# A layered graph network inside a six-part kernel: gathers of 784 unpadded chunks, products over pairs of chunk and target block

## The reference, cut to what matters

```python
dinv = where(deg > 0, deg ** -0.5, 0.0)
norm = dinv[row] * dinv[col]
for l in range(5):
    edge_fea = concatenate([edge_attr[:, 3:] @ ew1[l], edge_attr[:, 0:3] @ ew2[l]], axis=-1)
    msg = norm[:, None] * (h[row] + edge_fea)
    agg = segment_sum(msg, col, num_segments=n)
    h = relu(concatenate([h, agg], axis=1) @ mlp_w[l] + mlp_b[l])
    ...  # normalised over the nodes; relu but in the last layer
```

## Time and profile before

| | us |
|---|---|
| runs of the kernel before | 14183.71, 14226.25, 14222.39 |
| their median | 14222.39 |
| the profiled execution | 14220.56 |
| its span in the trace | 14218.8 |
| POOL busy | 7369.4 (52%) |
| PE busy | 7586.1 (53%) |
| DVE busy | 6529.1 (46%) |
| ACT busy | 1314.3 (9%) |
| gathers of the layers, first to last issue, layers 0 to 4 | 1365, 1273, 1282, 1276, 1280 |

### The profile page before, as it was taken

The page is one execution under the profiler, slowest core; times in us unless marked ns, Lnnn a source line. Parts: engine busy times, 40 slices in busy tenths (PEclk is TensorE's granted clock), DMA queues, the critical chain, the costliest instruction groups (busy, mean ns, idle before and its releaser), DMA issues. The chain is left out here.

```text
span 14218.8 us, 158198 instructions
## 1 busy us (share of the span) xinstructions
PE 7586.1 (53%) x34918; PEld 5503.2 (39%) x34919; DVE 6529.1 (46%) x18936; ACT 1314.3 (9%) x3588; POOL 7369.4 (52%) x7692
## 2 busy tenths in 40 slices
PE   0002355552139677765655465555554655378877
PEld 0002344431026444444544344444443444233355
DVE  7336544411015356654444344434443444345566
ACT  0000000001001100001000100010001000123342
POOL 5772466635740255564666566656665666445400
PEclk9999866675569788877776777677776766578988
DMA  1000233211000133322333233323332333211203
GB/s 58 20 1 1 71 91 91 82 43 48 2 7 21 57 81 83 82 73 63 88 87 87 67 87 87 87 69 86 88 87 67 85 88 87 58 21 21 23 11 102
DMA packets 518785, 873.35 MB, mean 61 GB/s; under 512 B 180375, under 2 KB 355656, under 8 KB 517579
## 3 DMA queue, kind: packets, MB, share of 16 engines
q0 software_dynamic: 323968, 674.90, 18.6%
q1 hardware_dynamic: 194635, 196.60, 4.4%
HBM read 771.76 MB, written 105.62 MB: 62 GB/s over the span
## 5 line engine op out<-in xcount | busy, mean ns | idle before, releaser
L308 POOL DMA_INDIRECT p_layers_place<-nodesC,p_layers_idx x4160 | 3942.5, 948 | 2937.6 <-issue 1573.7
L393 PE MATMUL p_layers_bank<-p_layers_hots,p_layers_place 128*128 128x128 f32 x16640 | 3366.7, 362 | 2863.4 <-DVE agg L379 1513.9
L393 PEld LDWEIGHTS p_layers_bank<-p_layers_hots,p_layers_place 128*128 128x128 f32 x16640 | 2869.0, 257 | 3452.7 <-issue 1933.9
L379 DVE TENSOR_TENSOR agg<-agg,p_layers_bank 128x256 f32 x4160 | 1751.5, 421 | 2282.3 <-issue 858.9
L369 DVE TENSOR_SCALAR p_layers_hots<-iota,p_msg_edges 128x128 f32<-128x128 f32 x3328 | 997.6, 363 | 759.9 <-issue 599.8
L308 POOL DMA_INDIRECT p_gather_rows<-xn,p_gather_idx x832 | 788.3, 947 | 822.7 <-ACT p_gather_idx L302 578.6
L263 POOL DMA_INDIRECT listC<-h x782 | 777.1, 994 | 526.1 <-issue 253.0
L393 PE MATMUL p_agg_bank<-p_agg_hot,p_gather_rows 128*128 128x128 f32 x3328 | 685.9, 374 | 594.2 <-DVE agg L379 372.9
L263 POOL DMA_INDIRECT listA<-h x782 | 812.7, 1039 | 344.4 <-issue 341.0
L263 POOL DMA_INDIRECT listD<-recD,rowD x512 | 493.1, 963 | 785.3 <-issue 785.3
L393 PEld LDWEIGHTS p_agg_bank<-p_agg_hot,p_gather_rows 128*128 128x128 f32 x3328 | 602.8, 271 | 677.9 <-issue 373.6
(11 more groups left out here) (387 smaller groups left out, 8125.2 us busy)
## 6 DMA issues: line engine op xcount, KB each, us to landing
p_layers_place<-nodesC,p_layers_idx POOLq DMA_INDIRECT x4160
nodesC<-p_layers_place SPq DMA_DIRECT2D x24, 896.0 KB, 4.7
part_y<-rows SPq DMA_DIRECT2D x21, 896.0 KB
agg<-part_y SPq DMA_DIRECT2D x18, 896.0 KB, 10.3
p_gather_rows<-xn,p_gather_idx POOLq DMA_INDIRECT x832
x<-p_ffn_acc SPq DMA_DIRECT2D x14, 896.0 KB, 4.1
listA<-h POOLq DMA_INDIRECT x782
listC<-h POOLq DMA_INDIRECT x782
```

What stands on the lines that cost most here:

```text
L308: nc.gpsimd.indirect_dma_start(out=self.rows[s][:, u, :], out_offset=None, in_=self.table, in_offset=bass.IndirectOffsetOnAxis(ap=self.idx ...
L379: nc.vector.tensor_tensor(to, to, prod, ALU.add).then_inc(self.added[u], 1)
L393: ins = nc.tensor.matmul(self.bank[u][:, f * P:(f + 1) * P], self.g.rows[s][:, u, f * P:(f + 1) * P], self.hot[s][:, u, :], start=True, st ...
```

## The change

In the message network alone:

- `PackedSort` takes the place of `Sort` for this list. The windows' edges follow each other without holes, which makes `NQ` = 784 chunks. A chunk may then hold edges of two windows, so the products go over pairs (chunk, window), of which there are again up to 832. `PackedSort` makes five tables in spare words of `rows`: each pair's window (`cw`), its slot among the 16 tiles of gathered chunks (`slots`), how many sets must have landed (`landed`), how many pairs must be copied before a set's slot is free (`freed`), and for the next step each pair's chunk and window (`pair_q`, `pair_w`). Each record's place gets its window times 128 added.
- `Spread`, in the first block of `messages`, spreads the places from chunks to pairs: 7 parts, each of a transpose and products of 832 columns on PE, and a comparison and a copy on DVE.
- `FromList` and `PairAggregate` run the layers. POOL's loop has 49 turns (784 gathers) and waits for `ready[s]`, which is now the end of a DMA. SP's loop issues that DMA (`give`: 128x4 source nodes into `idx[s]`, in layer 0 also the records' raw words) after it has waited for the slot, and tells ACT of landed sets (`relay`). ACT copies each pair's 128x260 from its slot to one of two halves of 4 (`near`), and in layer 0 makes the attribute product, which was DVE's. PE reads `near`. The loops of ACT, PE and DVE keep 52 turns.
- `edges` shrinks to the source nodes (128 x 784). 16 more scatters of the second graph's list stand beside the layer norm of `messages` (`NORM_D` 60 to 76), 16 fewer in the last part.

```diff
 NC2 = chunks_of(E2)
 FIRST_A = 128
 PARTS_C = (0, 160, 138)
-PART_D, NORM_D, FIRST_D, PER_D = 40, 60, 40, (80, 58, 58, 58)
+PART_D, NORM_D, FIRST_D, PER_D = 40, 76, 40, (80, 58, 58, 58)
 EVERY, RINGS = 8, 3
 RA, RC, RD = 3, 6, 2
+NQ = -(-E1T // SU) * SU
+PAIR_ROW, PAIR_SLOT, PAIR_LAND, PAIR_FREE = 32, NC1, 2 * NC1, 2 * NC1 + NC1 // U
...
+class PackedSort(Sort):
...
+    def __init__(self, sp, sh, T, key, rec, row, one, rows):
+        tables = rows[PAIR_ROW:PAIR_ROW + 1, :].bitcast(I32)
+        super().__init__(sp, sh, T, NQ, key, rec, row, tables[:, 0:NC1], one)
+        self.slots, self.landed = tables[:, PAIR_SLOT:PAIR_SLOT + NC1], tables[:, PAIR_LAND:PAIR_LAND + NC1 // U]
+        self.freed, self.work = tables[:, PAIR_FREE:PAIR_FREE + NQ // U], tables[:, PAIR_WORK:PAIR_WORK + NC1]
+        self.pair_q, self.pair_w = rows[:, PAIR_Q:PAIR_Q + NC1], rows[:, PAIR_W:PAIR_W + NC1]
...
+    def _tables(self, nc, dve, link):
+        sh, ends, row = self.sh, self.ends[:, 1:NT + 1], slice(PAIR_ROW, PAIR_ROW + 1)
+        last, cut, begin = (self.marks[:, n, :] for n in range(3))
...
+        link(nc.vector.tensor_scalar(self.len_j, self.len_i, P - 1, None, ALU.bitwise_and))
...
+        link(nc.vector.tensor_tensor(last, self.low, cut, ALU.add))
...
+        nc.vector.sem_inc(self.marked, 1)
...
+        dve.wait_ge(self.turned, START + 3)
+        link(nc.vector.tensor_copy(self.cols, self.sums[0:NT, 128:131]))
+        link(nc.vector.tensor_copy(self.split, self.cols[:, 1:2].to_broadcast([NT, P])))
+        link(nc.vector.tensor_scalar(self.ended, sh.chunkrow[0:NT, 0:NC1], self.cols[:, 0:1], None, ALU.is_ge))
+        link(nc.vector.tensor_scalar(self.begun, sh.chunkrow[0:NT, 0:NQ:U], self.cols[:, 2:3], None, ALU.is_ge))
+        nc.vector.sem_inc(self.after_done, 1)
...
+        dve.wait_ge(self.winsum, START + 2)
+        link(nc.vector.tensor_scalar(self.pair_w, self.wide[:, 0:NC1], float(NT - 1), float(P), ALU.min, ALU.mult))
+        link(nc.vector.tensor_scalar(self.cw, self.wide[row, 0:NC1], float(NT - 1), None, ALU.min))
+        nc.vector.sem_inc(self.rows_done, 1)
...
+        dve.wait_ge(self.winsum, START + 4)
+        link(nc.vector.scalar_tensor_tensor(self.pair_q, sh.chunkrow[:, 0:NC1], 1.0 / P, self.wide[:, 0:NC1], ALU.mult,
+                                            ALU.subtract))
+        nc.vector.sem_inc(self.rows_done, 1)
+        link(nc.vector.tensor_scalar(self.pair_q, self.pair_q, float(NQ - 1), None, ALU.min))
+        link(nc.vector.tensor_copy(self.work, self.pair_q[row, :]))
+        link(nc.vector.tensor_scalar(self.slots, self.work, SU - 1, None, ALU.bitwise_and))
+        link(nc.vector.tensor_scalar(self.landed, self.work[:, U - 1:NC1:U], 2, None, ALU.arith_shift_right))
+        link(nc.vector.tensor_scalar(self.landed, self.landed, 1.0, None, ALU.add))
...
+        dve.wait_ge(self.winsum, START + 5)
+        link(nc.vector.scalar_tensor_tensor(self.freed, sh.chunkrow[row, 0:NQ:U], 1.0 / P, self.wide[row, 0:NQ // U],
+                                            ALU.mult, ALU.add))
...
+    def _tables_pe(self, nc, pe):
...
+        for n, by in enumerate((sh.ones[0:NT, :], self.split)):
+            if n:
+                pe.wait_ge(self.rows_done, START + n)
+            for b in range(0, NC1, 512):
+                m = min(512, NC1 - b)
+                nc.tensor.matmul(self.wide[:, b:b + m], by, self.ended[:, b:b + m], start=True,
+                                 stop=True).then_inc(self.winsum, 1)
+        pe.wait_ge(self.rows_done, START + 2)
+        nc.tensor.matmul(self.wide[:, 0:NQ // U], self.split, self.begun, start=True, stop=True).then_inc(self.winsum, 1)
...
+class FromList(Gather):
...
+    def pool_set(self, nc, pool, it, s):
+        pool.wait_ge(self.ready[s], it * 16 + 16)
+        hold(pool)
+        for u in range(U):
+            nc.gpsimd.indirect_dma_start(
+                out=self.rows[s][:, u, :], out_offset=None, in_=self.table,
+                in_offset=bass.IndirectOffsetOnAxis(ap=self.idx[s][:, u:u + 1], axis=0)).then_inc(self.here[s], 16)
...
+class PairAggregate(Aggregate):
...
+    HALVES = 2
...
+        self.near = [sp.sb(f"near{h}", [P, U, TW]) for h in range(self.HALVES)]
...
+    def pe_set(self, nc, pe, it, s, edge_terms):
+        near, attr = self.near[s % self.HALVES], self.attr[s % self.HALVES]
+        pe.wait_ge(self.hot_ready, START + it * S + (s + 1))
+        for u in range(U):
+            pe.wait_ge(self.copied, START + it * SU + (s * U + u + 1))
+            pe.wait_ge(self.added[u], START + it * S + s)
+            if edge_terms:
+                pe.wait_ge(self.attr_made, START + it * SU + (s * U + u + 1))
+                pe.wait_ge(self.edge_added, START + it * SU + (s * U + u + 1))
+            for f in range(FB):
+                ins = nc.tensor.matmul(self.bank[u][:, f * P:(f + 1) * P], near[:, u, f * P:(f + 1) * P],
+                                       self.hot[s][:, u, :], start=True, stop=True)
...
             ins.then_inc(self.g.used, 1)
...
+    def act(self, nc, act, l, edge_terms, zero):
+        with act.Fori(0, self.turns) as i:
+            it = l * self.turns + i
+            land = numbers_of(nc, mybir.EngineType.Activation, self.land, i * S, S, NQ // U)
+            for s in range(S):
+                near, attr = self.near[s % self.HALVES], self.attr[s % self.HALVES]
+                slots = numbers_of(nc, mybir.EngineType.Activation, self.slots, i * SU + s * U, U, SU - 1)
+                act.wait_ge(self.g.used, START + it * SU + (s * U + AHEAD - (self.HALVES - 1) * U))
+                act.wait_ge(self.landed, (land[s] & 255) + (START + l * (NQ // U)))
+                for u, slot in enumerate(slots):
+                    nc.scalar.copy(near[:, u, :], self.flat[:, ds(slot * TW, TW)]).then_inc(self.copied, 1)
+                if edge_terms:
+                    act.wait_ge(self.copied, START + it * SU + (s * U + U))
+                    hold(act)
+                    for u, slot in enumerate(slots):
+                        nc.scalar.activation(attr[:, u, :], self.raw.rearrange("p t w -> p (t w)")[
+                            :, ds(slot * RC + 2, 4)], ACT.Identity, bias=zero[:, 0:1],
+                                             scale=near[:, u, D:D + 1]).then_inc(self.attr_made, 1)
...
+    def sp(self, nc, sp, l, edge_terms):
+        def relay(i, s):
+            sp.wait_ge(self.g.here[s], (l * self.g.turns + i) * (16 * U) + 16 * U)
+            hold(sp)
+            if edge_terms:
+                sp.wait_ge(self.raw_here[s], i * 16 + 16)
+                hold(sp)
+            nc.sync.sem_inc(self.landed, 1)
+        def give(i, s, done):
+            sp.wait_ge(self.copied, done + (START + l * NC1))
+            hold(sp)
+            if edge_terms:
+                sp.wait_ge(self.attr_made, done + START)
+                hold(sp)
+            sp.dma_start(self.g.idx[s], self.g.edges[:, ds(i * SU + s * U, U)]).then_inc(self.g.ready[s], 16)
+            if edge_terms:
+                sp.dma_start(self.raw[:, s * U:(s + 1) * U, :],
+                             self.listed[:, ds(i * SU + s * U, U), :]).then_inc(self.raw_here[s], 16)
+        for s in range(S):
+            if s == S - 1:
+                relay(0, 0)
+            give(0, s, 0)
+        with sp.Fori(1, self.g.turns) as i:
+            free = numbers_of(nc, mybir.EngineType.SP, self.free, i * S - (S - 1), S, NC1)
+            for s in range(S):
+                relay(i - 1 if s < S - 1 else i, (s + 1) % S)
+                give(i, s, free[s] & 1023)
+        for s in range(1, S):
+            relay(self.g.turns - 1, s)
...
                 normalise(l)
             clear(l)
-            with act.Fori(0, self.g.turns) as i:
-                for s in range(S):
-                    self.g.act_set(nc, act, l * self.g.turns + i, i, s)
+            self.a.act(nc, act, l, l == 0, self.zero)
...
@@ -1810,6 +2023,54 @@
         nc.vector.tensor_tensor(to, to, self.turn.rearrange("p (f n) -> p f n", f=FB), ALU.add).then_inc(self.added, 1)
...
+        self.numbered, self.flipped = sp.sem("numbered"), sp.sem("flipped")
+        self.made, self.taken = sp.sem("made"), sp.sem("taken")
+        self.parts = [(k, min(P, NQ - k)) for k in range(0, NQ, P)]
+    def pe(self, nc, pe):
+        def flip(n):
+            k, m = self.parts[n]
+            nc.tensor.transpose(self.turn[0:m, n % 2, :], self.numbers[:, k:k + m],
+                                self.sh.ident).then_inc(self.flipped, 1)
+        flip(0)
+        for n, (k, m) in enumerate(self.parts):
+            pe.wait_ge(self.made, START + 2 * n + 2)
+            if n + 1 < len(self.parts):
+                flip(n + 1)
+            for b in range(0, NC1, 512):
+                c = min(512, NC1 - b)
+                ins = nc.tensor.matmul(self.sums[:, b:b + c], self.turned[n % 2][0:m, :],
+                                       self.picks[n % 2][0:m, b:b + c], start=(n == 0),
```

(17 more changed lines are left out.)

167 lines of the change are left out of this document (123 added, 44 removed).

## The result

The changed kernel took 14792.91 us (median of four, 14741.26 to 14820.99) beside 14205.36 us for the kernel before: 1.041 of it, 95% interval 1.0374 to 1.0445. The forecast was 14312 us, with 14530 as the end of the range: right in sign, far too small in size. Two later comparisons gave 1.0445 (1.0417 to 1.0473) and 1.0432 (1.0386 to 1.0479).

The account below looks back on a forecast made before the run. POOL's stops for used sets and DVE's slow phases beside POOL's runs were taken as the bound. Profiled 14220.6 + 12 tables + 20 spread + 4 starts + 48 layers 1 to 4 + 7 layer 0 = 14312 us; range 13950 to 14530.

Parts of the forecast that it names:

- What bounds the kernel: Layers: gathered rows lie ready; POOL stops for want of used sets, DVE is slow at 0.3 pace during POOL's runs.
- The release and the stop: Layers 1 to 4: freeing a slot through copies and index DMA takes 3.75 us, making POOL's stop 4.9 us.
- The cycle, n = (g + 4.27) / 2.90: Layers 1 to 4: sets per POOL run n from stop g; at 4.9 us n = 3.16, a layer 1284 us.
- Layers 1 to 4: Gather layers after the first: 12 us more each, +48 in all, from -8 to +120, upper end +160.
- Layer 0: First gather layer, DVE relieved of the attribute product: +7 us, from -98 to +57.
- The tables: Some 25 DVE operations and a second row product on PE: +12 us, from 0 to 25.
- Spread: After the norm in the messages' first block, seven parts on PE, plus pick and sum: +20 us, from 11 to 24.
- The 16 scatters: Beside the messages' norm: 20 us of POOL, hidden behind its 40.9 us wait for the block's end.
- The last part: End of the kernel: gains nothing, since POOL is done there before the norm.
- C: Rival: slow slot release near 7 us, stop 6.5 us, 1323 us a layer, 14518 us in all; chance 0.22.
- B': Rival: DVE loses a fixed 0.51 us per gather, so fewer gathers give 14107 us; chance 0.15.
- D: Rival: ACT slowed like DVE, some 150 us more a layer, 15000; sign: PE waits for ACT's copies; chance 0.06.

Follow-up runs that it names:

- e1: Kernel before with each set's indices brought by SP's DMA instead of ACT's copy; 1.0004 of the kernel before, which took 10784 us in that sitting.
- e8: Kernel before with each set's indices brought by SP's DMA instead of ACT's copy; 1.0346 of the kernel before, which took 14294 us in that sitting.
- e18: The changed kernel again, in a sitting where the kernel before took 10767 us; 10494.17 us, 0.9745 of it.
- e16: Kernel before with fewer register instructions on DVE: places in a tile of their own, windows stored times 128; 0.9970 of the kernel before.

## Why the prediction was wrong, step by step

- *What bounds the kernel.* Right: gathered rows lie ready, DVE's slow phases beside POOL's runs set the time, and a longer stop costs. e1 against e8 and e18 show it from both sides.
- *The release and the stop.* Nearly right. The way was put at 3.75 us and is 3.0 in the cycle shown, the stop at 4.9 us and is 4.7 in the mean and 5.8 in the mean of those over 3 us.
- *The cycle, n = (g + 4.27) / 2.90.* This is the step that failed. For g = 4.9 it gave runs of 3.16 sets and 6.55 us a set: 62 stops a layer, 304 us. Measured are runs of 784 / 83 / 4 = 2.4 sets and 6.98 us a set: 82 stops, 387 us. The length of a stop was right, their number was not. I had let DVE keep its full pace for 7.1 us into a run and regain it 1 us after, whatever the stop, with 0.3 of its pace between. In the changed kernel the first slow instruction comes 5.0 us into a run (median; 7.0 before), DVE does next to nothing then in the cycle shown, and is back after 2.4 us. The longer stop thus buys too little work: 832 / 83 = 10.0 chunks in a cycle of 16.5 us against 832 / 101 = 8.2 in 12.7. That is 1.8 chunks more, 1.9 us of DVE's full pace, for 3.8 us. The fit was weak from the start: it met the 1272 us with the long stop of 3.1 us and n = 2.78, where the kernel before has a mean stop of 2.4 us and runs of 2.1 sets, so two errors cancelled there. The 0.3 had been fitted to that one stop, so it could say nothing about another. The cycle should have been fitted to two places with different stops, or its bound taken at zero pace: with 0 in place of 0.3, 4.40 n = g + 6.1 gives n = 2.5 and 196 x 6.96 = 1364 us, which is near what came. That is hindsight, not a model: the same would have given 1331 us for the kernel before, where it is 1278. The pace in the slow phase isn't one number, and the range had to reach from the one to the other. Why the slow phase comes sooner in the changed kernel stays open.
- *Layers 1 to 4*: 12 us each forecast, 90 measured. *Layer 0*: 7 forecast, 153 measured. I take it for the same term, with the way longer by ACT's attribute products and by the DMA of the raw words, which the prediction leaves out; no run takes these apart. The index DMA alone cost 100 us there in e8 (1465). The 0.57 us a set that DVE was to save there don't show.
- *The tables*: 12 forecast, 5 measured. *Spread*: 20 forecast, 14 measured.
- *The 16 scatters were not hidden.* I named POOL's 40.9 us wait as their cover and overlooked that DVE's norm stands beside them and crawls as long as they run. In the timeline of the changed kernel DVE is slow until 4884.65, and the norm's last work starts at 4908.97, 24.6 us after that of the earlier trace rows, 5.8 of it from a later start:

```profile
4884.65 0.17 DVE L970 TENSOR_SCALAR msg_norm_rstd<-msg_norm_mv 128x7 f32<-128x7 f32 x1 [5.67 <-remote]
...
4908.97 2.35 DVE L978 TENSOR_SCALAR msg_norm_xn<-msg_norm_x,msg_norm_mv,msg_norm_rstd 128x256 f32<-128x256 f32 x7
4928.37 0.06 DVE L1333 MEMSET p_layers_zero<- 128x1 f32 x1 [0.34 <-PEq L2451]
```

  e18 bears out that it is this slowness: the 16 scatters stand there too, DVE isn't slowed, and the norm's last work starts 2.6 us before that of e1 (3370.9 and 3373.5 us). The last part got the same 20 us back (its norm's last work starts 267.4 us after the last addition of layer 4, where it was 287.5), which I had put at nothing. The other 23 us that it gained I can't place.
- *The rivals.* C named the right mechanism, and as its price 51 us a layer, from a stop of 6.5 us. B' (a fixed loss per gather) is out, since 48 gathers fewer made the layers longer. D's mechanism is out: ACT's register instructions keep their 0.04 to 0.05 us beside POOL's runs. But the sign that the prediction gave for D did come: PE waits for ACT's copies 78 us in the 1300 shown, 92 us a layer, not "a few us". The prediction had PE's wait for its rows at nothing. As the layers grew by 90 us, this second way, from the landed row over SP and ACT to PE, is a rival for a part of them, and it is untested.

## What to carry to other kernels

When two engines throttle each other through a buffer, the latency of handing a slot back counts even if the data lie ready for microseconds: put nothing into that way (a DMA of 2 KB) that can be done ahead of the wait, and let the consumer's signal reach the producer directly. Work taken off an engine that looks busy need not pay: here neither the attribute product taken off DVE nor e16's 12% fewer records shows in the time. A cycle model fitted to one operating point should be tried with its weakest parameter at both ends before its slope is believed.
